# Splitting a shared expert block into three fp32r products of high and low parts, on a kernel of eight layers

## The chip, the cores and the metric

The kernel runs on one core of a Trainium2 chip. The metric is the device time of one execution in microseconds. Five engines matter: TensorE (PE; its weight loads are listed as PEld), VectorE (DVE), ScalarE (ACT), GpSimd (POOL) and SyncE (SP), which issues most of the transfers.

## What is computed

Four layers, each a gated attention and a gated feed-forward part, act on 2048 tokens (8 sequences of 256) of width 256. The change lies in the first feed-forward part: eight routed experts, two of them for each token, and a shared expert for every token.

```python
def _L0_ffn_ref(x, Wg, W1, b1, W2, b2, Ws1, bs1, Ws2, bs2):
    ...
    logits = xf @ Wg
    top_vals, top_idx = jax.lax.top_k(logits, TOP_K)
    top_w = jax.nn.softmax(top_vals, axis=-1)
    combine = jnp.zeros((T, N_EXPERTS), x.dtype).at[jnp.arange(T)[:, None], top_idx].add(top_w)
    h = jax.nn.relu(jnp.einsum('td,edf->tef', xf, W1) + b1)
    sparse = jnp.einsum('te,tef,efd->td', combine, h, W2)
    sparse = sparse + combine @ b2
    shared = jax.nn.relu(xf @ Ws1 + bs1) @ Ws2 + bs2
    out = sparse + shared
    ...
x = x + jnp.tanh(g_ffn[0]) * _L0_ffn_ref(_layernorm(x, axis=-1), ...)
```

Ws1 is 256x1024 and Ws2 1024x256. The kernel's line numbers below are those of the profile.

## The kernel before

Everything here happens in phase_experts with l = 0. Tokens are held in 16 tiles of 128, or 4 blocks of 512 (blk 0 to 3); x_tok holds the residual rows, xnT the normalised rows turned (width on the partitions, two halves k), xn_tok the normalised rows for the next part (in the buffer vbuf). The order of each engine is written out by hand, and semaphores join the engines.

1. The router's work, and on PE the shared expert for token blocks 0 and 1 (shared_block, L1503 and L1514).
2. The ring: 39 steps, each of 128 rows that are routed to one expert. In a step PE multiplies by the expert's first weights (L1557), ACT adds the bias and applies relu (L1442), PE turns the rows of the next step (L1546), ACT copies them (L1436), PE multiplies by the second weights (L1567), DVE adds a bias row (L1278), and POOL gathers the rows of a later step and scatters the result rows by indirect transfers (L1385, L1389). Steps 0 to 7 are written out, the others run in a loop.
3. Behind the ring PE runs the shared expert for token block 2, turns the normalised rows of blocks 0 and 1 (norm_T, L1580), runs the shared expert for token block 3, folds three small matrices for the next part, and turns the rows of blocks 2 and 3. ACT applies bias and relu to each of the eight hidden tiles f of 128 features by 512 tokens (L1423), which PE leaves in four PSUM banks in turn, and copies the turned rows out of PSUM (L355).
4. Meanwhile SP loads the scattered result rows back, a token block at a time (load_result, L1343), into two buffers gat, which lie in prob and probT. DVE's order is combine(0), norms(0), combine(1), norms(1), combine(2), combine(3), then shared_block and norms for block 2 and for block 3. combine (L1287) adds the weighted result rows to x_tok in eight passes of 128x256. shared_block adds the shared expert's rows from PSUM (L1261) and a bias row (L1266). norms takes statistics (L252 to L272), waits for POOL's power step (L277), and writes the normalised rows in four passes (L286).
5. POOL's order behind the ring is: three small products own_block for the fold (L1404), then the power step of norms for each block. A barrier ends the phase.

A matrix product of fp32 operands shows in the trace as two PE instructions, one of fp32r operands (a rounded 32-bit format) as one. The very last phase (L3171 to L3261) already works in three fp32r products: ACT writes a high part rounded to fp32r (L3189, L3196), DVE subtracts it from the full value to get the low part (L3213, L3218), and PE adds high times high, high times low and low times high (L3248 for the first layer, L3259 for the second).

Of the kernel before, what the change touches and what calls it, by code (L numbers as in the profile page):

```python
# [19 lines left out]
P = 128  # L20
NBATCH, SEQ, D = 8, 256, 256
T = NBATCH * SEQ
NT = T // P
BLK = 512
NB = T // BLK
KD = D // P
# [61 lines left out]
def decoder_kernel(nc, a, out):  # L88
    ctx = ExitStack()
    with ctx:  # L90
# [920 lines left out]
        def phase_experts(l, func, gi, keep, prefetch):  # L1011
# [78 lines left out]
            b2_sb = ts  # L1090

            def hidden(f):

                return ps[:, f % 4, 0:FINE]

            def normalised(blk, t):

                return xn_tok[:, blk * 4 + t, :]
            gat = [prob[:, :, :, :, :].rearrange("p a b c s -> p (a b c) s"), probT[:, :, :, :].rearrange("p a b s -> p (a b) s")]

# [21 lines left out]
            with nc.Block() as block:  # L1122
                @block.vector
                def _(dve):
# [149 lines left out]
                    def ring_step(s, v, k, last):  # L1274
                        dve.wait_ge(y_full[v], k + 1)
                        dve.wait_ge(y_st[v], k * 16)
                        dve.wait_ge(ld_b[v], k * 32 + 32)
                        dve.tensor_tensor(y_sb[v], ps[:, 4 + v, 0:D], b2_sb[:, v, :], ALU.add).then_inc(y_out[v], 1)  # L1278

                    def combine(blk):  # L1280
# [94 lines left out]
                def _(pool):  # L1375
# [11 lines left out]
                    def scatter(s):  # L1387
                        pool.wait_ge(y_out[s % 2], s // 2 + 1)
                        pool.indirect_dma_start(a["yg"], bass.IndirectOffsetOnAxis(dst_row[:, s:s + 1], 0), y_sb[s % 2], None).then_inc(y_st[s % 2], 16)  # L1389

                    pool.wait_ge(sent, 16)
                    pool.wait_ge(link, marks["indexed"])
# [4 lines left out]
                    for s in range(steps):  # L1397
                        if s + 3 < steps:
                            pool.wait_ge(g_full, s + 2)
                            gather(s + 3)  # L1400
                        scatter(s)
                    if shared:
                        for i in range(3):
                            ins = pool.tensor_tensor(own_block[i].rearrange("p (j c) -> p j c", c=HD), rep[:, i, :].unsqueeze(1).broadcast_to([P, GH, HD]),  # L1404
                                                     hmask[:, :].unsqueeze(2).broadcast_to([P, GH, HD]), ALU.mult)
                        ins.then_inc(wbd, 1)
                    for blk in range(NB):
                        nrm.power(pool, blk, 0)

                @block.scalar  # L1410
                def _(act):
# [26 lines left out]
                    def ring_step(s, v, k, last):  # L1438
                        act.wait_ge(ld_b[v], k * 32 + 32)
                        for f in range(NF):  # L1440
                            act.wait_ge(h_full, (s + lead) * NF + (f + 1))
                            act.activation(hs[:, f, :], hidden(f), func, bias=b1_sb[:, v, f:f + 1]).then_inc(h_in, 1)  # L1442
                        if not last:
                            rows_in(s + 1)

                    def norm_T(blk):
# [19 lines left out]
                    for blk in range(NB):  # L1466
                        if blk % 2 == 0:
                            shared_block(lead + steps + blk // 2, hT)
                        if shared and blk == 2:
# [8 lines left out]
                def _(pe):  # L1478
# [19 lines left out]
                    def shared_block(blk, u, hT):  # L1498
# [9 lines left out]
                        for tp in range(2):  # L1508
                            wait(pe, s_in, blk * 2)
                            for t in range(2):  # L1510
                                for f in range(NF):
                                    if tp == 0 and t == 0:
                                        pe.wait_ge(h_in, u * NF + (f + 1))
                                    ins = pe.matmul(ps[:, 4 + tp, t * D:(t + 1) * D], hT[:, f, (2 * tp + t) * P:(2 * tp + t + 1) * P],  # L1514
                                                    w2[0][:, f, :], start=(f == 0), stop=(f == NF - 1))
                            ins.then_inc(s_full, 1)

# [103 lines left out]
                    for blk in range(NB):  # L1621
                        if shared and blk % 2 == 0:
                            shared_block(lead + blk // 2, lead + steps + blk // 2, hT)
                        if shared and blk == 2:
# [1773 lines left out]
```

## Time and profile before

| | us |
|---|---|
| median of 3 runs | 1590.52 |
| lowest and highest | 1587.04, 1593.61 |
| profiled execution, its own time | 1590.82 |
| its span in the profile | 1588.3 |
| PE busy | 1393.3 (88%) |
| weight loads busy | 1125.8 (71%) |
| DVE busy | 698.4 (44%) |
| ACT busy | 653.1 (41%) |
| POOL busy | 486.8 (31%) |

The busy shares are averages over stages with different limits. In the profile the ring runs from about 312 to 597 us, and the part behind it, up to the barrier, from 597 to 664 us. All times below are microseconds from the start of the span.

### The profile page before, as it was taken

What the parts mean: (1) busy time and instruction counts of PE and PEld (TensorE: products, weight loads), DVE (VectorE), ACT (ScalarE), POOL (GpSimd) and SP (SyncE); (2) the same over time, 40 slices, a digit from 0 to 9 for tenths busy, and PEclk for the clock granted to TensorE, in tenths of its full rate; (3) what the DMA queues carried; (4) which work ended last, traced back from release to release, by engine and by line L of the source; (5) the groups of instructions that cost most, each with busy time, mean ns of one, the idle gap of its engine ahead of it and who ended that gap; (6) DMA issues with size and microseconds to landing.
All of it is one profiled execution on the core that took longest, in us unless ns stands there. A gap on an engine that the chain in (4) does not pass through costs nothing. (4 is left out here: it accounts for less than half of the span.)

```text
span 1588.3 us, 29051 instructions
## 1 busy us (share of the span) xinstructions
PE 1393.3 (88%) x9586; PEld 1125.8 (71%) x9587; DVE 698.4 (44%) x2242; ACT 653.1 (41%) x1466; POOL 486.8 (31%) x551
## 2 busy tenths in 40 slices
PE   4999978999999999799997899948588898686598
PEld 3666756699999996577776799945456777555587
DVE  4666725300000006277743300046654564459575
ACT  3354533244444442246662344433343444323352
POOL 4456531022222211213411022225237534031330
PEclk9899998999999999879998999978699999888799
DMA  8500006366666643000005465620137873010000
GB/s 280 163 2 1 2 1 218 117 197 201 198 203 195 205 152 119 7 14 15 15 8 150 163 212 189 209 66 1 36 133 228 285 222 113 1 53 1 1 26 26
DMA packets 114126, 175.84 MB, mean 111 GB/s; under 512 B 20555, under 2 KB 90845, under 8 KB 113513
## 3 DMA queue, kind: packets, MB, share of 16 engines
q1 hardware_dynamic: 103855, 146.35, 29.3%
q0 software_dynamic: 10176, 28.24, 4.9%
q8 instruction: 57, 0.93, 0.3%
q14 instruction: 38, 0.31, 0.1%
HBM read 135.16 MB, written 39.35 MB: 110 GB/s over the span
## 5 line engine op out<-in xcount | busy, mean ns | idle before, releaser
L1442 ACT ACTIVATE kT<-ps,b_sb 128x128 f32<-128x128 f32 x312 | 114.8, 368 | 155.6 <-PE ps L1557 134.7
L718 ACT ACTIVATE wbuf<-ps 128x512 f32<-128x512 f32 (+1 forms) x256 | 123.6, 542 | 85.6 <-PE ps L963 85.2
L1557 PEld LDWEIGHTS ps<-qT,wbuf 128*128 128x128 f32 x1248 | 145.4, 192 | 3.9 <-issue 1.9
L1557 PE MATMUL ps<-qT,wbuf 128*128 128x128 f32 x1248 | 145.7, 275 | 1.7 <-issue 1.7
L1567 PE MATMUL ps<-L0f_second,kT 128*128 x624 | 141.1, 379 | 0.0
L277 POOL TENSOR_TENSOR sm<-sm,mhalf 128x4 f32<-128x4 f32 (+1 forms) x40 | 45.0, 1124 | 292.2 <-DVE sm L272 292.2
L1567 PEld LDWEIGHTS ps<-L0f_second,kT 128*128 128x128 f32 x624 | 115.5, 190 | 14.1
L963 PE MATMUL ps<-nmT_r,sel_r 32*128 32x256 f32 (+1 forms) x512 | 110.9, 429 | 0.0
L765 DVE CUSTOM_DVE_ANT_0 ps<-ps,ts 128x128 f32<-128x128 f32 (+1 forms) x256 | 83.1, 391 | 44.3 <-PE ps L939 44.2
L768 DVE TENSOR_REDUCE nmax<-ps 128x2 f32<-128x512 f32 x128 | 80.5, 684 | 32.8 <-PE ps L939 32.7
L1968 ACT ACTIVATE kT<-ps,b_sb 128x128 f32<-128x128 f32 x152 | 55.6, 368 | 72.8 <-PE ps L2055 62.8
L355 ACT ACTIVATE xnT<-ps 128x512 f32<-128x512 f32 x64 | 36.4, 595 | 116.5 <-PE ps L332 63.8
L1385 POOL DMA_INDIRECT qT<-expert_rows,rowt x39 | 38.0, 974 | 149.0 <-PE ps L1546 106.4
L939 PE MATMUL ps<-hbuf,qT 32*128 32x512 f32 (+1 forms) x256 | 72.3, 687 | 3.4 <-POOL hbuf L613 1.2
L2055 PEld LDWEIGHTS ps<-qT,wbuf 128*128 128x128 f32 x608 | 70.9, 192 | 3.1 <-ACT qT L1962 1.5
L2055 PE MATMUL ps<-qT,wbuf 128*128 128x128 f32 x608 | 71.3, 275 | 1.6 <-ACT qT L1962 1.1
L959 PE MATMUL ps<-qT,hbuf 32*128 32x256 f32 (+1 forms) x512 | 72.4, 386 | 0.0
L1278 DVE TENSOR_TENSOR oT<-ps,ts 128x256 f32<-128x256 f32 x20 | 8.5, 425 | 139.8 <-PE ps L1567 139.8
L2065 PE MATMUL ps<-wbuf,kT 128*128 x304 | 68.8, 379 | 0.0
L959 PE MATMUL ps<-stage,hbuf 32*128 32x256 f32 (+1 forms) x512 | 68.2, 374 | 0.2 <-ACT nmT_r L675 0.2
L623 POOL TENSOR_SCALAR_AFFINE_SELECT wbuf<-wbuf 128x256 f32<-128x256 f32 x128 | 49.9, 411 | 57.4 <-ACT wbuf L718 55.5
L939 PE MATMUL ps<-hbuf,stage 32*128 32x512 f32 (+1 forms) x256 | 67.0, 569 | 0.0
(455 smaller groups left out, 3146.0 us busy)
## 6 DMA issues: line engine op xcount, KB each, us to landing
wbuf<-in_L_w SPq DMA_DIRECT2D x66, 1024.0 KB, 5.1
tree_rows<-rt SPq DMA_DIRECT2D x3, 3151.0 KB, 23.2
prob<-tree_rows SPq DMA_DIRECT2D x69, 137.0 KB, 3.7
tree_outputs<-probT SPq DMA_DIRECT2D x69, 128.0 KB
L0f_second<-in_L_w SPq DMA_DIRECT2D x8, 1024.0 KB, 11.5
ts<-in_L_b SPq DMA_DIRECT2D x58, 128.0 KB, 3.0
wbuf<-in_L_rec SPq DMA_DIRECT2D x3, 2048.0 KB, 9.3
expert_rows<-vbuf SPq DMA_DIRECT2D x2, 2048.0 KB, 12.3
```

Of the source, the lines that this page charges most:

```text
L718: act.activation(PT[:, k, :, q0:], ps[:, a_bank("ST", b, k), :].rearrange("p (h s) -> p h s", h=2)[:, :, q0:], ACT.Exp, scale=scale).then_ ...
L765: ins = dve.tensor_tensor_reduce(out=bank[:, e, 0:kk], in0=bank[:, e, 0:kk], in1=seen[:, SEQ - kk:SEQ], scale=-1.0, scalar=BIG, op0=ALU.ad ...
L768: ins = dve.tensor_reduce(nmax[:, b % 2, qt, h:h + 2], bank[:, :, 0:keys(qt)], AXX, ALU.max, negate=True)
L939: ins = pe.matmul(bank[:, :, 0:kk], qTb[blk % 2][r, g, u * SEQ + qt * P:u * SEQ + (qt + 1) * P], kmb[blk % 2][r, :, g, u * SEQ:u * SEQ + k ...
L959: pe.matmul(out, kmb[blk % 2][r, e, g, u * SEQ + kt * P:u * SEQ + (kt + 1) * P], qTb[blk % 2][r, g, u * SEQ + q0:(u + 1) * SEQ], start=Tru ...
L963: ins = pe.matmul(out, sel_r[r, h:h + 1].broadcast_to([2 * HD, P]), nmT_r[b % 2][r, q0:], start=False, stop=True)
L1442: act.activation(hs[:, f, :], hidden(f), func, bias=b1_sb[:, v, f:f + 1]).then_inc(h_in, 1)
L1557: ins = pe.matmul(hidden(f), first[v][:, kk, f * P:(f + 1) * P], xgT[:, kk, :], start=(kk == 0), stop=(kk == KD - 1))
L1567: ins = pe.matmul(ps[:, 4 + v, 0:D], hs[:, f, :], second[:, ds(e, 1), f * D:(f + 1) * D][:, 0, :], start=(f == 0), stop=(f == NF - 1))
L1968: act.activation(hs[:, f, :], hidden(f), func, bias=b1_sb[:, v, f:f + 1]).then_inc(h_in, 1)
L2055: ins = pe.matmul(hidden(f), first[v][:, kk, f * P:(f + 1) * P], xgT[:, kk, :], start=(kk == 0), stop=(kk == KD - 1))
L2065: ins = pe.matmul(ps[:, 4 + v, 0:D], hs[:, f, :], second[:, ds(e, 1), f * D:(f + 1) * D][:, 0, :], start=(f == 0), stop=(f == NF - 1))
```

## The change

For the shared expert on token blocks 2 and 3 alone, shared_block on PE and ACT is replaced by split_block. Each fp32 product becomes three fp32r products: high weights with high rows, high weights with low rows, low weights with high rows, 48 of 512 columns in the first layer and 96 of 256 columns in the second.

- The weights' high parts (hi_room, in prob and probT) are written by ACT in ring steps 2 to 5, the low parts by DVE in the same steps, over the weights themselves (wbuf 0).
- The high rows of block 2 are written by ACT in ring step 6, and the low rows by POOL behind the scatter of step 10 (low_rows(0)). Those of block 3 follow behind the ring: ACT behind the eight tiles of block 2, POOL behind the power step of norms(0) (low_rows(1)).
- For each hidden tile ACT writes the full value into one of four raw buffers and then its high part (hh), and POOL subtracts to get the low part (hl). PE's second layer waits for hid_lo, a tile at a time, and ACT waits for it before it writes a raw buffer again.
- On POOL low_hidden(0), the eight subtractions for block 2, stands ahead of the own_block products and of the first power step; low_hidden(1) stands ahead of the power step of norms(2).
- gat moves from prob and probT to the buffer of the ring's first weights (wbuf 1).

```diff
+            hi_room = nc.alloc_sbuf_tensor_at(f"{n}high", [P, 4096], F32R, offset=places["prob"])[:, :]
+            (hi1, lo1) = (x[:, 0:2048].rearrange("p (k f) -> p k f", k=KD) for x in (hi_room, wbuf_r[0]))
+            (hi2, lo2) = (x[:, 2048:4096].rearrange("p (f d) -> p f d", f=NF) for x in (hi_room, wbuf_r[0]))
+            hh, hl = (x.rearrange("p (f t) -> p f t", f=NF) for x in (wbuf_r[2], hbuf_r))
+            raw = attw[:, 0].rearrange("p w k n -> p (w k n)").rearrange("p (i t) -> p i t", i=4)
+            xh = [x.rearrange("p (k t) -> p k t", k=KD) for x in (rounded("rowsF", 4 * D, 1024), rounded("qT", 0, 1024))]
+            xl = [x.rearrange("p (k t) -> p k t", k=KD) for x in (rounded("stage", 0, 1024), rounded("kT", 0, 1024))]
...
-            gat = [prob[:, :, :, :, :].rearrange("p a b c s -> p (a b c) s"), probT[:, :, :, :].rearrange("p a b s -> p (a b) s")]
+            gat = [wbuf[:, 1, v * 2048:(v + 1) * 2048].rearrange("p (t d) -> p t d", d=D) for v in range(2)]
...
                         dve.tensor_tensor(y_sb[v], ps[:, 4 + v, 0:D], b2_sb[:, v, :], ALU.add).then_inc(y_out[v], 1)
+                        if isinstance(s, int) and 2 <= s < 6:
+                            q = chunk(s - 2)
+                            dve.wait_ge(w_hi, s - 1)
+                            dve.tensor_tensor(wbuf_r[0][:, q], wbuf[:, 0, q], hi_room[:, q], ALU.subtract).then_inc(w_lo, 1)
...
+                    def low_rows(i):
+                        pool.wait_ge(x_hi, i + 1)
+                        pool.tensor_tensor(xl[i], xnT[:, :, block_of(i)], xh[i], ALU.subtract).then_inc(x_lo, 1)
+
+                    def low_hidden(i):
+                        for f in range(NF):
+                            pool.wait_ge(hid_hi, i * NF + f + 1)
+                            pool.tensor_tensor(hl[:, f, :], raw[:, f % 4, :], hh[:, f, :], ALU.subtract).then_inc(hid_lo, 1)
...
                         scatter(s)
+                        if s == 10:
+                            low_rows(0)
                     if shared:
+                        low_hidden(0)
                         for i in range(3):
...
                     for blk in range(NB):
                         nrm.power(pool, blk, 0)
+                        if blk == 0:
+                            low_rows(1)
+                        elif blk == 1:
+                            low_hidden(1)
...
+                        if isinstance(s, int) and 2 <= s < 6:
+                            q = chunk(s - 2)
+                            act.wait_ge(s_full, 2 * lead)
+                            act.activation(hi_room[:, q], wbuf[:, 0, q], ACT.Identity).then_inc(w_hi, 1)
+                        if isinstance(s, int) and s == 6:
+                            act.activation(xh[0], xnT[:, :, block_of(0)], ACT.Identity).then_inc(x_hi, 1)
+
+                    def split_block(i):
+                        for f in range(NF):
+                            act.wait_ge(h_full, (lead + steps + i) * NF + (f + 1))
+                            wait(act, hid_lo, i * NF + f - 3)
+                            act.activation(raw[:, f % 4, :], ps[:, f % 4, :], func, bias=col("L0_bs1", f)).then_inc(h_in, 1)
+                            act.wait_ge(h_in, (lead + steps + i) * NF + (f + 1))
+                            act.activation(hh[:, f, :], raw[:, f % 4, :], ACT.Identity).then_inc(hid_hi, 1)
+                        if i == 0:
+                            act.activation(xh[1], xnT[:, :, block_of(1)], ACT.Identity).then_inc(x_hi, 1)
...
-                            shared_block(lead + steps + blk // 2, hT)
+                            split_block(blk // 2)
...
+                    def split_block(i):
+                        u = lead + steps + i
+                        pe.wait_ge(x_lo, i + 1)
+                        pe.wait_ge(w_lo, 4)
+                        for f in range(NF):
+                            if f >= 4:
+                                pe.wait_ge(h_in, u * NF + (f - 3))
+                            for k in range(KD):
+                                for j, (w, x) in enumerate(((hi1, xh[i]), (hi1, xl[i]), (lo1, xh[i]))):
+                                    ins = pe.matmul(ps[:, f % 4, :], w[:, k, f * P:(f + 1) * P], x[:, k, :],
+                                                    start=(k == 0 and j == 0), stop=(k == KD - 1 and j == 2))
+                            ins.then_inc(h_full, 1)
+                        for tp in range(2):
+                            pe.wait_ge(s_in, (lead + i) * 2)
+                            for t in range(2):
+                                for f in range(NF):
+                                    if tp == 0 and t == 0:
+                                        pe.wait_ge(hid_lo, i * NF + (f + 1))
+                                    for j, (h, w) in enumerate(((hh, hi2), (hh, lo2), (hl, hi2))):
+                                        ins = pe.matmul(ps[:, 4 + tp, t * D:(t + 1) * D], h[:, f, (2 * tp + t) * P:(2 * tp + t + 1) * P],
+                                                        w[:, f, :], start=(f == 0 and j == 0), stop=(f == NF - 1 and j == 2))
                             ins.then_inc(s_full, 1)
...
-                            shared_block(lead + blk // 2, lead + steps + blk // 2, hT)
+                            split_block(blk // 2)
```

In the prediction block 0 and block 1 of the split are token blocks 2 and 3, the first and the second behind the ring; combine and norms are numbered by token block.

## Rows read from the trace of the kernel before

**Rows 1.** Stretches: busy us of PE, PEld, DVE, ACT, POOL (instructions), granted clock, DMA.
```profile
597.20:625.00 27.80, 27.76 (x98) 18.44 (x99) 16.71 (x55) 5.50 (x8) 4.14 (x6) 1.00 0.53 170
...
661.60:663.70 2.10, 1.97 (x8) 1.57 (x8) 0.06 (x1) 0.60 (x1) 0.00 (x0) 0.50 0.00 0
1487.40:1490.80 3.40, 3.39 (x8) 2.72 (x9) 0.00 (x0) 0.43 (x1) 3.40 (x2) 0.52 0.00 0
1490.90:1499.70 8.80, 8.80 (x40) 7.28 (x39) 5.27 (x6) 8.28 (x14) 3.81 (x2) 1.00 0.00 0
```

**Rows 2.** Timeline of PE behind the ring: start, us, instruction, count, [idle before].
```profile
597.24 13.97 PE L1503 MATMUL ps<-xnT,wbuf 128*128 128x512 f32 x32 [0.61 <-DVE oT L1278]
...
624.86 1.04 PE L1580 MATMUL ps<-ident,vbuf 128*128 128x128 f32 x8
...
627.14 13.90 PE L1503 MATMUL ps<-xnT,wbuf 128*128 128x512 f32 x32
...
661.71 1.97 PE L1580 MATMUL ps<-ident,vbuf 128*128 128x128 f32 x8 [2.59 <-DVE vbuf L286]
```

**Rows 3.** Timeline of PE in the last phase, in three products.
```profile
1526.38 0.40 PE L3259 MATMUL ps<-wbuf_r,wbuf_r 128*128 128x256 f32 x2
...
1535.01 0.40 PE L3248 MATMUL ps<-ctxT_r,wbuf_r 128*128 x1
...
1545.92 0.40 PE L3259 MATMUL ps<-wbuf_r,wbuf_r 128*128 128x256 f32 x2
```

**Rows 4.** Timeline: ACT behind the ring; ACT and DVE in the last phase.
```profile
599.23 0.69 ACT L1423 ACTIVATE hbuf<-ps,cols 128x512 f32<-128x512 f32 x1 [5.65 <-PE ps L1503]
...
1497.44 0.69 ACT L3194 ACTIVATE hbuf<-ps,cols 128x512 f32<-128x512 f32 x1
...
1498.83 0.69 DVE L3218 TENSOR_TENSOR hbuf_r<-hbuf,wbuf_r 128x512 fp32r<-128x512 f32 x1 [0.67 <-ACT wbuf_r L3196]
```

**Rows 5.** Groups of POOL instructions by shape: count | busy us, mean ns | idle before.
```profile
L634 POOL TENSOR_SCALAR xs<-x_tok,sm 128x256 f32<-128x256 f32 x32 | 38.9, 1222 | 1.7
...
L613 POOL TENSOR_SCALAR hbuf<-ctxT,sel 128x512 f32<-128x512 f32 x14 | 21.8, 1573 | 55.2 <-PE ps L963 47.7 <-POOLq L114 7.5
...
L2140 POOL TENSOR_TENSOR probT<-rowsF,bmask 128x512 f32<-128x512 f32 x4 | 5.1, 1268 | 6.3 <-SPq L2131 6.3
```

**Rows 6.** Timeline of POOL, then of DVE, at one place of the last phase.
```profile
1515.28 2.38 POOL L3171 TENSOR_TENSOR vbuf<-vbuf,rowsF 128x1024 f32 x1
1517.62 2.59 POOL L3171 TENSOR_TENSOR x_tok<-x_tok,rowsF 128x1024 f32 x1
...
1515.49 5.00 DVE L305 SCALAR_TENSOR_TENSOR x_tok<-ts,sm,x_tok 128x256 f32 x2 [0.35 <-POOL sm L277]
```

**Rows 7.** Timeline of POOL and DVE at the start of the third attention.
```profile
1076.79 1.26 POOL L2140 TENSOR_TENSOR probT<-rowsF,bmask 128x512 f32<-128x512 f32 x1 [6.31 <-SPq L2131]
...
1076.81 1.53 DVE L2186 TENSOR_SCALAR rowsA<-rowsA,gates 128x512 f32<-128x512 f32 x1 [7.69 <-PEq L114]
```

**Rows 8.** Timeline of POOL and DVE behind the ring.
```profile
598.36 1.11 POOL L1404 TENSOR_TENSOR attw<-rep,hmask 128x128 f32<-128x128 f32 x3
...
605.53 3.38 DVE L1287 SCALAR_TENSOR_TENSOR x_tok<-prob,r,x_tok 128x256 f32<-128x256 f32 x8 [8.44 <-DMA prob<-expert_outputs]
...
612.55 1.38 DVE L286 TENSOR_SCALAR vbuf<-x_tok,sm 128x256 f32<-128x256 f32 x4 [1.16 <-POOL sm L277]
...
620.81 1.38 DVE L286 TENSOR_SCALAR vbuf<-x_tok,sm 128x256 f32<-128x256 f32 x4 [1.13 <-POOL sm L277]
...
654.89 0.88 DVE L1261 SCALAR_TENSOR_TENSOR x_tok<-ps,gates,x_tok 128x256 f32<-128x256 f32 x2 [5.11 <-PE ps L1514]
```

**Rows 9.** Timeline: ACT and POOL in a ring step; ACT rounding weights in a later phase.
```profile
358.30 3.44 ACT L1442 ACTIVATE kT<-ps,b_sb 128x128 f32<-128x128 f32 x8 [3.54 <-PE ps L1557]
...
347.33 0.97 POOL L1385 DMA_INDIRECT qT<-expert_rows,rowt  x1 [2.32 <-PE ps L1546]
...
1450.54 1.06 ACT L2988 ACTIVATE wbuf_r<-wbuf 128x1024 fp32r<-128x1024 f32 x1
```

More of the change, by code:

```diff
@@ L1090, in phase_experts, with chunk, block_of @@
             b2_sb = ts
+            w_hi, w_lo, x_hi, x_lo = (psem(n + x) for x in ("w_hi", "w_lo", "x_hi", "x_lo"))
+            hid_hi, hid_lo = psem(n + "hid_hi"), psem(n + "hid_lo")
+            hi_room = nc.alloc_sbuf_tensor_at(f"{n}high", [P, 4096], F32R, offset=places["prob"])[:, :]
[5 more added lines that the diff above has]
+            xl = [x.rearrange("p (k t) -> p k t", k=KD) for x in (rounded("stage", 0, 1024), rounded("kT", 0, 1024))]
+            def chunk(j):
+                return slice(j * 1024, (j + 1) * 1024)
+            def block_of(i):
+                return slice((lead + i) * BLK, (lead + i + 1) * BLK)
             def hidden(f):
@@ L1515, in shared_block @@
                                                     w2[0][:, f, :], start=(f == 0), stop=(f == NF - 1))
+                            ins.then_inc(s_full, 1)
+                    def split_block(i):
[19 more added lines that the diff above has]
+                                                        w[:, f, :], start=(f == 0 and j == 0), stop=(f == NF - 1 and j == 2))
                             ins.then_inc(s_full, 1)
```

## The prediction

> **What bounds the kernel now.** I read the page first (which engine is busiest), then the stretch that the change rewrites, engine by engine in order of time, then the one other place that already multiplies in high and low parts, and last the rows where POOL and VectorE (DVE) work at once. TensorE (PE) sets the time through the routed ring and through the shared block of the first token block behind it: that block's two layers follow each other without a gap [rows 2] at a granted clock of 1.00 [rows 1], and DVE's addition to x_tok then waits for PE [rows 8]. So an instruction saved on PE there counts, as long as PE is not made to wait. Between the two shared blocks that is close: PE must turn the normalised rows of blocks 0 and 1, and DVE finishes those of block 1 at 620.81 + 1.38 = 622.2 [rows 8], only 2.7 us before PE's first block ends at 624.9 [rows 2]. DVE is the engine next in line, and this change leans on DVE's neighbour.
>
> **PE's work.** One fp32 block takes 624.86 - 597.24 = 27.6 us [rows 2]. The last phase has the same shapes in three fp32r products: its first layer takes 1545.92 - 1535.01 = 10.9 us, and its second, in the stretch where nothing waits, 1535.01 - 1526.38 = 8.63 us for 24 of its 32 groups, so 0.36 us a group and 11.5 us in all [rows 3]. A new block is 22.4 us, a gain of 5.2 us each, 10.4 us for both. That is all there is to win.
>
> **What moves into the ring costs nothing.** ACT writes the high weight parts in steps 2 to 5 and the first high rows in step 6, 128x1024 each; such a pass took 1.06 us and ACT waits 3.54 us in every step [rows 9]. DVE's four low weight parts are 128x1024; a 128x512 subtraction took 0.69 us [rows 4], so 1.4 us at most, and DVE does nothing else in a step but one addition (queued behind it: the next addition, a step later). On POOL low_rows(0) stands behind scatter 10 and ahead of gather 14; POOL idles 2.32 us before a gather [rows 9], the subtraction is some 2.4 us, and the gathered rows are read over a step later. If that cover failed, one gather late by 0.1 us would be the price. The result rows now land in the first layer's weight buffer, which the ring has left when those loads are issued; their place in SP's queue is the same. The waits on x_lo (first block) and w_lo are long met.
>
> **POOL's subtractions, block 0.** Times are on the clock of the profile before. PE starts at 597.24 and gives a tile of hidden rows every 10.9 / 8 = 1.36 us. ACT started 0.25 us after the first tile was complete (599.23, four instructions of 0.44 after 597.24 [rows 2, 4]); from the first ACT pass to the subtraction it is 1498.83 - 1497.44 = 1.39 us [rows 4]. So subtraction f can start at 597.24 + 1.36 + 0.25 + 1.39 = 600.24 plus 1.36 f. No POOL row writes fp32r. The nearest is POOL's f32 two-input pass of this size, 1.27 us; the far ends are 1.57 us (one input and a pointer) and 1.22 us for half the size, 2.44 us [rows 5]. None below 1.27 at this size, so no gain. I take 1.26, since DVE's fp32r and f32 passes of one size cost alike, and keep 2.44 for the range. Alone, POOL would then keep up: subtraction 7 ends at 611.0, PE has reached its group 7 at 610.7, and next to nothing is lost.
>
> **POOL against DVE.** It is not alone. While POOL added rows at 1515.28 and 1517.62, two DVE passes of 0.42 us took 5.00 us: each ended when a POOL pass had ended, one pass after the other, and the second POOL pass was 0.21 us longer than the first [rows 6]. A DVE tensor_scalar started beside a POOL pass of 1.26 us took 1.53 us, 0.29 past its end [rows 7]. So two-input DVE passes and DVE's scalar passes from SBUF to SBUF take turns with POOL. DVE's combine(0) (8 such passes) starts at 605.53, when its rows land [rows 8], as subtraction 3 ends. From there a POOL pass and a DVE pass alternate, 1.26 + 0.28 = 1.54 us a pair: subtraction 7 ends at 605.58 + 4 x 1.54 = 611.7. Behind it on POOL stand the three own_block products (0.37 each [rows 8]), three more turns, 1.95 us; combine(0) ends at 614.0, not 608.9. The power step of norms(0) stands behind all this on POOL; with the same distance as before (612.55 - 608.91) it ends at 617.6. Right behind it in POOL's queue is low_rows(1), 2.4 us (128x1024 [rows 6]), ready by then; POOL starts it before DVE starts (1515.28 against 1515.49 behind a power step [rows 6]), and DVE's normalising passes wait: they end at 617.6 + 2.4 + 1.4 = 621.4, not 613.9. From there to the normalised rows of block 1 it is as before, 622.19 - 613.93 = 8.3 us [rows 8]: 629.7, which is 7.5 us late.
>
> The Trainium skill's "SBUF — State Buffer", section "Who interferes with whom", says the same of that pair: DVE's second port is shared with GpSimd under an exclusive lock held for a whole instruction, and passes with two SBUF inputs or in a 2-port mode take it. It speaks against this change; by it the sum is the +1.1 us below, without it the -7.9 us of the second rival, and the rows side with it.
>
> **PE again.** Block 0's first layer ends at 608.2; group 7 waits for 611.8, then 0.36 + 8.63: block 0 ends at 620.8, 4.1 us early. Then PE waits for DVE until 629.7. After a wait of 2.59 us the turning took 1.97 us against 1.04 [rows 2], at a granted clock of 0.50 [rows 1], the lower of the two levels, so block 1 starts at 631.7, not 627.14. In the last phase the low level lasted for 8 products of 0.43 instead of 0.23 us [rows 1]; 1.6 us in all; part of it falls on the turning, so I take 0.7 us, an estimate. First layer to 643.3; subtraction f at 631.7 + 0.7 + 3.0 + 1.36 f. DVE is then in combine(2) and combine(3) (629.7 to 638.7 with turns) and in shared_block's four two-input additions; about six subtractions are stretched from 1.36 to 1.54 us, so the last ends at 644.9 + 1.26 + 0.8 = 646.9. PE: 647.0 + 0.36 + 8.63 = 656.0. Before, it was 27.6 us after 627.14, 654.8, and DVE's last addition at 654.89. The power of norms(2) now stands behind the subtractions (it ends at 649), but PE needs those rows only after 656. **Sum: +1.1 us** (4.1 us gained, 8.6 lost between the blocks, 3.4 gained in block 1), handed on unchanged, since everything behind waits for this. Profiled 1590.82 + 1.1 = 1591.9; the median of the runs lies 0.3 lower: 1591.6.
>
> **Rivals.** *Slower: POOL writes fp32r slowly.* The decider is the time of one 128x512 subtraction. At 1.57 us, the same steps give subtraction 7 at 614.2, block 1's normalised rows at 632.8, PE's end at 661.9, +7 us. At 2.0 us, subtraction 7 at 617.7, rows at 637, block 1's last subtraction at 660.5, its end at 669.6, +14.7 us or 1605; it passes 8 us at about 1.6. For it: POOL's pointer forms show such rates, and four raw buffers make ACT wait for POOL. Against: the two-input form does not. *Faster: DVE is not held.* If POOL and DVE overlap freely, power 0 waits only for the own_block products (612.2, not 611.5), block 1's rows are ready at 622.9, PE goes on at 624, and block 1 ends 13.9 + 9.0 us later at 646.9: -7.9 us, 1582.6. Against: every row of rows 6 and 7. *In between*, DVE may win more turns, or the normalising passes go first: 1 to 3 us less, in my own range.
>
> **How the numbers follow.** The forecast, 1588 to 1597 (one POOL pass between 1.2 and 1.5 us, the clock 1.5 us either way), gets 0.69; the slower rival 0.15, spread over 1597 to 1610; the faster one 0.11, 1582 to 1588; 0.05 for a delay not foreseen. The measurement tells 0.5%, 8 us: below 1582.6 lies 0.04, above 1598.5 lies 0.12, within 0.84. The range cuts the outer parts of both rivals: 1584 to 1601.
>
> **What would show it.** Right: POOL's subtractions at 1.25 us and stretched from the fifth on; combine(0) some 8 us long instead of 3.4; PE idle about 7 us ahead of block 1's turning, which runs at the lower clock level; PE's blocks without their waits at 22.4 us. Wrong: a subtraction of over 1.6 us, DVE passes of 0.42 us beside POOL, ring steps longer than before, or a first layer not at 1.36 us a tile.

## The result, and the profile after

| | before | after |
|---|---|---|
| median of 20 runs each, us | 1590.55 | 1593.61 |
| lowest and highest | 1584.94, 1593.63 | 1585.73, 1599.21 |
| ratio, 95% interval | | 1.0022 [1.0012, 1.0032] |
| profiled execution, its own time | 1590.82 | 1594.28 |
| its span | 1588.3 | 1592.4 |
| POOL busy | 486.8 | 517.8 |

The changed kernel is no faster: slower by 3.5 us, between 1.9 and 5.1, which lies inside the 0.5% that the prediction called no change. The prediction, 1591.6 us within 1584 to 1601, holds the time, but some 2 us of the difference come from a place that it did not look at.

For all that follows, *the stage* runs from the first product of the shared block behind the ring to VectorE's first instruction behind the barrier. In the kernel before that is 597.24 [rows 2] to 667.75, 70.5 us; its end there:

```profile
667.75 0.35 DVE L825 TENSOR_SCALAR rowsA<-rowsA,gates 128x256 f32<-128x256 f32 x1 [6.09 <-PEq L114]
```

The timeline of the kernel after, PE, then POOL, then DVE (start, us, engine, line, operation, count, [idle time before and who ended it]):

```profile
597.71 0.47 PE L1579 MATMUL ps<-rowsF_r,L0f_high 128*128 128x512 f32 x1 [0.56 <-issue]
...
612.11 0.39 PE L1589 MATMUL ps<-L0f_high,wbuf_r 128*128 128x256 f32 x1 [0.76 <-POOL hbuf_r L1418]
...
629.40 1.97 PE L1655 MATMUL ps<-ident,vbuf 128*128 128x128 f32 x8 [7.15 <-DVE vbuf L286]
...
600.80 11.26 POOL L1418 TENSOR_TENSOR hbuf_r<-attw,wbuf_r 128x512 fp32r<-128x512 f32 x8 [1.94 <-ACT wbuf_r L1494]
612.02 1.67 POOL L1436 TENSOR_TENSOR attw<-rep,hmask 128x128 f32<-128x128 f32 x3
616.52 1.05 POOL L277 TENSOR_TENSOR sm<-sm,mhalf 128x4 f32<-128x4 f32 x1 [2.83 <-DVE sm L272]
617.56 2.39 POOL L1413 TENSOR_TENSOR kT_r<-xnT,qT_r 128x1024 fp32r<-128x1024 f32 x1
...
606.14 7.83 DVE L1307 SCALAR_TENSOR_TENSOR x_tok<-wbuf,r,x_tok 128x256 f32<-128x256 f32 x8 [8.54 <-DMA wbuf<-expert_outputs]
...
617.61 3.47 DVE L286 TENSOR_SCALAR vbuf<-x_tok,sm 128x256 f32<-128x256 f32 x4 [1.17 <-POOL sm L277]
...
627.96 1.38 DVE L286 TENSOR_SCALAR vbuf<-x_tok,sm 128x256 f32<-128x256 f32 x4 [1.13 <-POOL sm L277]
...
656.07 0.88 DVE L1277 SCALAR_TENSOR_TENSOR x_tok<-ps,gates,x_tok 128x256 f32<-128x256 f32 x2 [3.97 <-PE ps L1589]
...
668.97 0.35 DVE L825 TENSOR_SCALAR rowsA<-rowsA,gates 128x256 f32<-128x256 f32 x1 [6.13 <-PEq L114]
```

Read it against [rows 8]. combine(0), 3.38 us before, takes 7.83 us; it starts while POOL is in its eight subtractions and ends 0.3 us behind POOL's last small product. Normalising block 0, 1.38 us before, takes 3.47 us: the first of its four passes ends only 0.15 us behind low_rows(1) on POOL, which ends at 619.96. So block 1's rows are ready at 629.3, and PE stands idle for 7.15 us before it turns them. What the faster products won is given back in that wait and in the low clock behind it: PE's second block ends 58.2 us into the stage, before it was 57.5. The stage ends after 668.97 - 597.71 = 71.3 us, 0.8 us longer than before.

The granted clock belongs to it. Stretches of the kernel after (us, busy us of PE, PEld, DVE, ACT and POOL with their counts, granted clock, DMA):

```profile
597.71:608.68 10.97, 10.97 (x49) 9.09 (x49) 2.54 (x3) 9.07 (x14) 8.59 (x7) 1.00 0.65 196
608.68:621.20 12.52, 11.76 (x97) 11.55 (x96) 11.14 (x23) 2.47 (x4) 8.45 (x8) 1.00 0.41 122
...
629.40:631.00 1.60, 1.60 (x8) 1.60 (x9) 1.56 (x5) 0.45 (x1) 0.00 (x0) 0.50 0.00 0
631.00:634.60 3.60, 3.60 (x11) 2.83 (x10) 3.53 (x9) 1.38 (x3) 0.00 (x0) 0.50 0.00 0
```

Block 2's products take 10.97 and 12.52 us at a granted clock of 1.00, with 0.76 us of waiting: 22.7 us instead of the 27.6 of [rows 2]. The clock falls during the wait and is at 0.50, the lower level of 1.2 GHz, until about 634.6; the second block's first layer takes 643.69 - 631.02 = 12.7 us instead of 11.

### The profile page after: what moved, and what is told of

Read it like the earlier page. It is cut to its first block and busy times, and to the rows that moved or that the text cites. A ratio compares the mean times of both kernels' runs of the same rounds, so it can differ in the third digit from the quotient of the medians.

```text
span 1592.4 us, 29301 instructions
## 1 busy us (share of the span) xinstructions
PE 1386.7 (87%) x9682; PEld 1133.0 (71%) x9683; DVE 714.6 (45%) x2246; ACT 669.0 (42%) x1488; POOL 517.8 (33%) x569
## 5 line engine op out<-in xcount | busy, mean ns | idle before, releaser
L2130 PEld LDWEIGHTS ps<-qT,wbuf 128*128 128x128 f32 x608 | 70.9, 192 | 3.1 <-ACT qT L2037 1.5
L2130 PE MATMUL ps<-qT,wbuf 128*128 128x128 f32 x608 | 71.3, 275 | 1.6 <-ACT qT L2037 1.1
L623 POOL TENSOR_SCALAR_AFFINE_SELECT wbuf<-wbuf 128x256 f32<-128x256 f32 x128 | 50.2, 415 | 57.0 <-ACT wbuf L718 55.2
L959 PE MATMUL ps<-stage,hbuf 32*128 32x256 f32 (+1 forms) x512 | 68.2, 374 | 0.2 <-ACT nmT_r L675 0.2
```

The source lines that it names most:

```text
L959: pe.matmul(out, kmb[blk % 2][r, e, g, u * SEQ + kt * P:u * SEQ + (kt + 1) * P], qTb[blk % 2][r, g, u * SEQ + q0:(u + 1) * SEQ], start=Tru ...
L2130: ins = pe.matmul(hidden(f), first[v][:, kk, f * P:(f + 1) * P], xgT[:, kk, :], start=(kk == 0), stop=(kk == KD - 1))
```

## The experiments

One table first. The wait of ScalarE is the one for the last store in the tree phase, which comes up in the second half. Where no ratio stands, there was one profiled execution, and only the parts read from its trace are compared, since single times of one kernel lie up to 13.5 us apart. Each ratio is to the kernel before as it was run beside that kernel, with medians of 1588.97 to 1590.55 us; so the medians of two rows are not to be subtracted.

| kernel | stage, us | ScalarE's wait | median, us | ratio to before |
|---|---|---|---|---|
| before | 70.5 | 3.66 | 1590.55 | |
| after | 71.3 | 5.72 | 1593.61 | 1.0022 [1.0012, 1.0032] |
| e1, no subtractions for block 2 | 67.4 | 5.73 | | |
| e2, low rows early | 69.2 | 5.23 | | |
| e3, own_block products late | 70.9 | 5.35 | | |
| e6, fills for subtractions | 67.3 | 5.08 | | |
| e7, VectorE subtracts | 67.6 | 5.55 | | |
| e9, new order, POOL subtracts | 64.8 | 5.53 | | |
| e8, new order, VectorE subtracts | 63.2 | 5.42 | 1587.78 | 0.9979 [0.9965, 0.9993] |
| b_order, before in the new order | 68.2 | 3.67 | 1588.48 | 0.9992 [0.9976, 1.0007] |
| e10, subtractions earlier | 60.7 | 5.17 | 1583.78 | 0.9959 [0.9944, 0.9973] |
| e11, the ring's additions alone | 70.6 | 3.61 | 1590.66 | 1.0005 [0.9990, 1.0020] |
| b_eps, other last bits | 70.5 | 3.68 | 1591.03 | 1.0006 [0.9990, 1.0023] |
| e12, as e10, 62 instructions more | 62.5 | 3.67 | 1581.20 | 0.9950 [0.9931, 0.9968] |

### Is it the subtractions on POOL? (e1)

```diff
-                        low_hidden(0)
...
-                                    for j, (h, w) in enumerate(((hh, hi2), (hh, lo2), (hl, hi2))):
+                                    for j, (h, w) in enumerate(((hh, hi2), (hh, lo2), (hl if i else hh, hi2))):
```

> Left out: POOL's eight subtractions for the first split block; PE's second layer there waits for the high parts alone and multiplies the high part once more in place of the low part. Everything else is as in the changed kernel, whose stage (first product of the first split block to the first DVE instruction behind the barrier) took 71.3 us, against 70.5 before the change. Theory (POOL's reading passes and DVE's two-input passes take turns): combine(0) takes 3.4 us instead of 7.8, the power step of norms(0) comes 3.6 us behind its end, the normalising passes still take 3.5 us behind low_rows(1), the normalised rows of block 1 are ready 4.4 us earlier, and the stage takes 66.8 us, within 0.7. Rival (DVE is late for another reason, its rows landing late or PE's own pace): 70.5 to 71.3 us.

ScalarE, too, no longer waits for POOL before it writes a raw buffer of that block. Timeline of that kernel, DVE, POOL and PE:

```profile
606.50 3.38 DVE L1307 SCALAR_TENSOR_TENSOR x_tok<-wbuf,r,x_tok 128x256 f32<-128x256 f32 x8 [8.66 <-DMA wbuf<-expert_outputs]
613.52 3.48 DVE L286 TENSOR_SCALAR vbuf<-x_tok,sm 128x256 f32<-128x256 f32 x4 [1.17 <-POOL sm L277]
...
613.48 2.39 POOL L1413 TENSOR_TENSOR kT_r<-xnT,qT_r 128x1024 fp32r<-128x1024 f32 x1
...
625.32 1.97 PE L1655 MATMUL ps<-ident,vbuf 128*128 128x128 f32 x8 [3.83 <-DVE vbuf L286]
```

combine(0) takes 3.38 us again, as in [rows 8], and the stage 67.4 us: as the theory had it. The 2.1 us that low_rows(1) takes from the normalising passes are still there.

### Which POOL pass costs what? (e2, e3)

e2 issues low_rows(1) ahead of power(0):

```diff
+                        if blk == 0:
+                            low_rows(1)
                         nrm.power(pool, blk, 0)
-                        if blk == 0:
-                            low_rows(1)
-                        elif blk == 1:
+                        if blk == 1:
                             low_hidden(1)
```

> One move on POOL: low_rows(1) stands ahead of the power step of norms(0) instead of behind it, in the gap in which POOL waited 2.8 us for DVE's statistics. Theory: DVE's four normalising passes of block 0 take 1.4 us instead of 3.5, nothing else is held, block 1 starts 2.1 us earlier and the stage takes 69.2 us instead of 71.3. Rival (the hold only moves, because the subtraction now runs into combine(0) or into the power step): 70.8 to 71.5 us.

```profile
615.13 2.58 POOL L1413 TENSOR_TENSOR kT_r<-xnT,qT_r 128x1024 fp32r<-128x1024 f32 x1
...
619.72 1.38 DVE L286 TENSOR_SCALAR vbuf<-x_tok,sm 128x256 f32<-128x256 f32 x4 [1.16 <-POOL sm L277]
...
629.43 1.97 PE L1655 MATMUL ps<-ident,vbuf 128*128 128x128 f32 x8 [5.71 <-DVE vbuf L286]
```

Beside the statistics the same POOL pass holds almost nothing (only the first two-input pass there, L260, waits for its end: 0.81 us instead of 0.17), normalising takes 1.38 us again, and the stage is 69.2 us, on the number expected. e3 moves the three own_block products from behind low_hidden(0) to behind power(2):

> One move on POOL: the three own_block products stand behind the power step of norms(2), where the fold still gets them in time, instead of between the subtractions and the first power step. Theory: three turns less for combine(0), 7.8 us become 6.0, the rows of block 1 are ready 1.8 us earlier, the stage takes 69.5 us. Rival (the subtractions alone set the end of combine(0)): 71.0 us or more.

```profile
600.48 11.11 POOL L1418 TENSOR_TENSOR hbuf_r<-attw,wbuf_r 128x512 fp32r<-128x512 f32 x8 [1.96 <-ACT wbuf_r L1495]
...
605.42 7.63 DVE L1307 SCALAR_TENSOR_TENSOR x_tok<-wbuf,r,x_tok 128x256 f32<-128x256 f32 x8 [8.15 <-DMA wbuf<-expert_outputs]
```

A miss. combine(0) is 0.2 us shorter and the stage 0.3, not 1.8. Here the subtractions end at 611.59 and combine(0) at 613.05; its last three passes take 0.47 us each. In the kernel after they took 0.62, in turns with the three products of 0.58 us. A turn with a POOL pass about as short as the DVE pass costs little; I had charged each turn as if it came on top.

### Does POOL hold VectorE because it is busy, or because it reads? (e6)

```diff
-                            pool.tensor_tensor(hl[:, f, :], raw[:, f % 4, :], hh[:, f, :], ALU.subtract).then_inc(hid_lo, 1)
+                            pool.memset(hl[:, f, :].bitcast(F32), 0.0).then_inc(twice, 1)
+                            pool.wait_ge(twice, i * NF + f + 1)
+                            pool.memset(hl[:, f, :].bitcast(F32), 0.0).then_inc(hid_lo, 1)
```

> Left out: every subtraction of POOL for the hidden tiles; in its place two fills of the same 128x512 low part with zeros, one after the other, some 1.1 us together by the fills of the trace (942 ns for 1024 columns), so POOL is as busy and in the same order, but reads nothing. If DVE's two-input passes are held only by a POOL pass that reads, combine(0) takes 3.4 to 4.5 us (the three own_block products still read), the rows of block 1 are ready 3 to 4 us earlier, and the stage takes 67 to 68 us instead of 71.3. If any POOL pass holds them: combine(0) 6.5 us or more and 70 us or more.

```profile
608.36 0.53 POOL L1421 MEMSET hbuf_r<- 128x512 f32 x1
609.13 0.53 POOL L1419 MEMSET hbuf_r<- 128x512 f32 x1 [0.25 <-ACT wbuf_r L1497]
...
607.64 3.38 DVE L1308 SCALAR_TENSOR_TENSOR x_tok<-wbuf,r,x_tok 128x256 f32<-128x256 f32 x8 [8.48 <-DMA wbuf<-expert_outputs]
```

POOL writes through that stretch, two fills in every 1.36 us, and combine(0) takes 3.38 us. That the fills are short is not the reason: beside the own_block products, which read and take 0.58 us, VectorE's passes took 0.62 us in the kernel after, and 0.47 without them in e3. So here a POOL pass that reads SBUF holds VectorE's two-input passes, one that only writes does not. The Trainium skill, "SBUF — State Buffer", section "Who interferes with whom", draws the same line, between GpSimd instructions that read SBUF and those that only write it; here it is 7.83 against 3.38 us.

### The same work on the other engine (e7)

VectorE does the eight subtractions of block 2, four in its idle time ahead of combine(0) and four between its passes, and low_rows(1) in its wait for power(1).

```diff
+                    for f in range(4):
+                        low(0, f)
+                    combine(0, [(0, f) for f in range(4, NF)])
+                    norms(0)
+                    combine(1)
+                    norms(1, (low_rows,))
```

> The same subtractions on the other engine. VectorE makes the eight low hidden parts of the first split block (four in its idle time ahead of combine(0), four between the passes of combine(0)) and the low rows of the second block (in its wait for power(1)); POOL makes only the low hidden parts of the second block. Stage = from the first product of the split block behind the ring to VectorE's first instruction behind the barrier (before 70.5 us, after 71.3). Theory (POOL's reading passes alternate with VectorE's two-input passes): a subtraction alone on VectorE takes half of the 1.22 us that its 128x1024 one in the ring takes, some 0.65 us, so combine(0) and its four subtractions take 3.4 + 2.6 = 6 us, normalising takes 1.4 us again, TensorE waits 3 to 4 us instead of 7.15 for the second block's rows, and the stage takes 67.2 to 68.5 us, 3 to 4 under that of after. Rival (the work is too much for VectorE, the hold was no loss): combine(0) with its subtractions as long as before the move, 7.8 us or more, stage 70 us or more.

```profile
609.21 0.68 DVE L1302 TENSOR_TENSOR hbuf_r<-attw,wbuf_r 128x512 fp32r<-128x512 f32 x1
609.82 0.87 DVE L1316 SCALAR_TENSOR_TENSOR x_tok<-wbuf,r,x_tok 128x256 f32<-128x256 f32 x2
...
614.80 1.38 DVE L286 TENSOR_SCALAR vbuf<-x_tok,sm 128x256 f32<-128x256 f32 x4 [1.16 <-POOL sm L277]
...
625.41 1.97 PE L1671 MATMUL ps<-ident,vbuf 128*128 128x128 f32 x8 [3.93 <-DVE vbuf L286]
```

As expected: a subtraction of 128x512 is 0.68 us on VectorE, combine(0) with four of them 5.6 us (605.63 to 611.2) instead of 7.83 without any, and the stage 67.6 us. Here the engine that lent its neighbour the work and then waited for it in turns paid more than the work. PE still waits 3.93 us, so the question became whether it must turn rows there at all.

### The order of the stage (b_order, e9, e8, e10)

Nothing that the second shared block reads is written by the turning of blocks 0 and 1, so nothing asks for the turning between the blocks. In these kernels PE and ACT run both blocks and turn only then:

```diff
+                    for i in range(2):
+                        split_block(i)
                     for blk in range(NB):
-                        if shared and blk % 2 == 0:
-                            split_block(blk // 2)
```

b_order does that alone, in the kernel before, with shared_block.

> The kernel before with TensorE's and ScalarE's order alone changed: both fp32 shared blocks behind the ring one after the other, then the turning. Theory: before, TensorE loses only the 2 us of turning between the two blocks and some of their clock, so the two blocks end after 2 x 27.6 = 55.2 us instead of 57.6, and the stage takes 67.5 to 69 us instead of 70.5: 1.5 to 3 us faster. It says what of the new order's gain belongs to the products of high and low parts. Rival (turning is paid again behind the blocks): 70 us or more, no change.

```profile
599.70 13.97 PE L1503 MATMUL ps<-xnT,wbuf 128*128 128x512 f32 x32 [0.61 <-DVE oT L1278]
...
654.87 1.04 PE L1580 MATMUL ps<-ident,vbuf 128*128 128x128 f32 x8
...
667.91 0.35 DVE L825 TENSOR_SCALAR rowsA<-rowsA,gates 128x256 f32<-128x256 f32 x1 [6.09 <-PEq L114]
```

The stage ran from 599.70 to 667.91, 68.2 us, 2.3 us less, as expected. Over the whole time that stays inside the interval. e9 has the new order with POOL subtracting (VectorE makes low_rows(1), runs combine(1) in its wait for power(0), and adds block 2's rows ahead of combine(2)):

> The order of the stage changed: TensorE and ScalarE run the second split block right behind the first and turn the rows of the token blocks only then; VectorE runs combine(1) inside its wait for power(0), the adds of the first split block ahead of normalising(1), and the low rows of the second block; POOL still makes both blocks' low hidden parts. Stage as for the other runs (before 70.5 us, after 71.3). Theory: TensorE's wait of 7.15 us and its low clock behind it are gone, but POOL's subtractions now hold combine(0) (about 7.8 us instead of 3.4) and combine(2) and (3) too, so VectorE becomes the engine that sets the end: stage 65 to 68 us. Rival (the holds cost nothing once TensorE doesn't wait): as the kernel in which VectorE subtracts, 60 to 62 us.

```profile
625.56 10.86 POOL L1435 TENSOR_TENSOR hbuf_r<-attw,wbuf_r 128x512 fp32r<-128x512 f32 x8
...
630.02 5.27 DVE L286 TENSOR_SCALAR vbuf<-x_tok,sm 128x256 f32<-128x256 f32 x4
...
662.51 0.35 DVE L825 TENSOR_SCALAR rowsA<-rowsA,gates 128x256 f32<-128x256 f32 x1 [6.13 <-PEq L114]
```

64.8 us, nearer to the theory than to its rival: VectorE's normalising is held again, 5.27 us instead of 1.38, now by the second block's subtractions. e8 gives all sixteen to VectorE:

> The order of the run in which POOL subtracts, but VectorE makes all sixteen low hidden parts itself, between the passes of combine(0), (2) and (3). Theory: TensorE runs both split blocks without a wait (2 x 22.4 = 45 us), VectorE's chain (combines 13.5, subtractions in the way some 8, statistics and normalising 4 x 4, adds 7) ends about together with it, and the last block's adds, statistics, normalising, turning and the barrier take their 13 us: stage 60 to 62 us, 8 to 10 under before, some 1582 us against 1590.5. Rival (VectorE becomes the bound with sixteen more passes): stage 64 to 67 us and no gain over the run in which POOL subtracts.

```profile
634.76 0.39 PE L1605 MATMUL ps<-L0f_high,wbuf_r 128*128 128x256 f32 x1 [0.96 <-DVE hbuf_r L1302]
...
661.22 0.35 DVE L825 TENSOR_SCALAR rowsA<-rowsA,gates 128x256 f32<-128x256 f32 x1 [6.13 <-PEq L114]
```

63.2 us, between the two: PE's second layer waits for VectorE's last subtractions, which I had put behind passes that nobody was waiting for. e10 makes these first:

```diff
+                    def second_lows():
+                        for f in range(4):
+                            low(1, f)
+                        dve.wait_ge(sadd, 2 * lead + 2)
+                        combine(2, [(1, f) for f in range(4, NF)], 1)
...
+                    norms(1, (lambda: shared_block(2), second_lows))
+                    combine(3)
+                    norms(2, (lambda: shared_block(3),))
```

> As the kernel in which VectorE makes all sixteen low hidden parts, whose second block's second layer waited until 637.4 us for the last of them: here the second block's eight come right after the adds of the first split block, the last four one behind each pass of combine(2), ahead of combine(3); and the last block's adds lie in the wait for power(2). Theory: TensorE runs the second block in 22.4 us again instead of 27.4, VectorE's chain loses one wait for a power (1.2 us), and the stage takes 60 to 61.5 us instead of 63.2 (before 70.5): the whole time 2 to 3 us under that kernel's, if the tree phase is the same. Rival (VectorE's chain alone sets the end, the order of its passes doesn't matter): 62.5 us or more.

Stretches of that kernel, PE first; they are its two blocks:

```profile
597.58:620.40 22.82, 22.47 (x142) 20.39 (x143) 17.11 (x45) 11.53 (x17) 4.04 (x5) 1.00 0.55 165
620.40:643.00 22.60, 22.60 (x148) 20.70 (x147) 20.59 (x59) 10.59 (x16) 1.32 (x2) 1.00 0.13 44
```

Behind them, PE's first turning and VectorE's first instruction behind the barrier:

```profile
643.08 1.04 PE L1672 MATMUL ps<-ident,vbuf 128*128 128x128 f32 x8
...
658.29 0.35 DVE L825 TENSOR_SCALAR rowsA<-rowsA,gates 128x256 f32<-128x256 f32 x1 [6.13 <-PEq L114]
```

Two blocks of 22.6 to 22.8 us with next to no gap (0.35 us in the first), at a granted clock of 1.00, and a stage of 60.7 us, within the expected 60 to 61.5. That is 9.8 us under the kernel before, where the order alone, with fp32 blocks, gave 2.3. PE's two blocks take 45.5 us there and 55.2 in b_order, so on PE the products of high and low parts are worth 9.7 of the 10.4 us that the prediction counted. At the end of the stage 7.5 us of it are left. The 7.5 are not theirs alone: e10 also changed VectorE's order, which was not tried with fp32 blocks.

### Where the other 2 us went (e11, b_eps, e12)

The stage accounts for 0.8 of after's 3.5 us. The barriers of the profile show where the rest is: of the later phases only the second feed-forward part, the tree phase, is over half a microsecond longer. It is a ring of row loads and stores, and its length swings: 243.8 to 247.1 us in the four kernels with plain fp32 blocks, 245.0 to 250.6 in the first nine with split blocks. One wait at its end is steadier. Timeline of ScalarE, which waits for the last store, in the kernel before:

```profile
1322.38 1.09 ACT L2734 ACTIVATE qT<-ps 128x512 f32<-128x512 f32 x2 [3.66 <-DMA tree_outputs<-probT]
```

and after:

```profile
1326.98 1.08 ACT L2809 ACTIVATE qT<-ps 128x512 f32<-128x512 f32 x2 [5.72 <-DMA tree_outputs<-probT]
```

It is 3.6 to 3.7 us in those four kernels, 5.1 to 5.7 in those nine. e11 keeps the change's additions to the ring and runs the blocks in plain fp32 on the old weights; b_eps is the kernel before with every activation changed in its last bits (EPS = 1.1e-5).

> The change's additions to the ring alone (the high and low parts of the weights and of the first block's rows are made there, the gather's room is moved), with the two shared blocks behind the ring in plain fp32 on the weights as they were, so that every number is that of the kernel before; no subtractions of hidden parts. Theory (the ring hides its additions; the part of the change's time that the stage doesn't explain comes from the tree phase, and there from something else than these additions): ring as long as before, stage 70.5 +- 0.5 us, tree phase 243.8 to 244.5 us, whole time as before within its interval. Rival A (the additions, or the program that they lengthen, slow the tree phase): tree phase 246 us or more, 2 to 3 us slower. Rival B (the additions lengthen the ring): the ring over 0.5 us longer.

> The kernel before with the norms' constant at 1.1e-5 instead of 1e-5: every instruction the same, every activation behind the first norm changed in its last bits, as the three products change them too. Theory D (the change's longer tree phase comes from other last bits, through which rows go to other places): tree phase 245 us or more, and 15 us instead of 13.5 from the last load of a step's rows to the gather of the third tree. Theory P (it comes from the program, not from the numbers): tree phase 243.8 to 244.5 us, 13.5 us, whole time as before.

Both took the time of the kernel before within their intervals, and waited 3.61 and 3.68 us at that spot. So it is neither the additions nor the numbers. e11's ring was as long as before and its stage 70.6 us; its tree phase of 247.1 us would by itself have spoken for its rival A, and that of b_eps, about 244.8 us, lies between what its two theories expected. So the phase's length is no measure; the wait is.

What the nine share is 192 more PE instructions (9682 products and 9683 weight loads against 9586 and 9587) and two more waits. Transfer queues of the kernel after, from 1 us into that wait to its end (queue, kind: packets, MB, share):

```profile
q1 hardware_dynamic: 394, 1.13, 68.2%
q8 instruction: 1, 0.02, 2.1%
```

In all nine a packet of the instruction queue moves in that stretch, in none of the four. e12 tests that by length alone:

```diff
+                    for _ in range(122):
+                        pe.wait_ge(gate_in, 8)
```

> As the fastest kernel so far (stage 60.7 us, 1583.78 us), with 122 met waits, which make 62 instructions, at the end of TensorE's queue in the first experts phase, where it waits some 5 us for the barrier. What is open: at the end of the tree phase ScalarE waits 5.1 to 5.7 us for the last store in all nine kernels with split blocks and 3.6 to 3.7 us in the four without, and only in the nine does a packet of the instruction queue move between that store and its landing. These nine have 194 more instructions for TensorE (14907 instead of 14713, and 57 packets, so some 258 a packet); with 62 more the shift is 256, nearly a whole packet, and the packet should move some 4 to 5 us earlier, to where it moved before. Theory (that packet holds the last store or the loads around it up): the wait is 3.6 to 3.7 us again, no such packet moves in that stretch, 13.5 to 13.7 us from the last load of a step's rows to the third gather instead of 14.95, the whole time 1 to 2 us less. Rival (the packet is only a companion): the packet moves away, the wait stays over 5 us. The 62 instructions lie beside the other engines' end of the phase: stage 60.7 +- 0.5 us.

Timeline of ScalarE in e12:

```profile
1317.55 1.08 ACT L2828 ACTIVATE qT<-ps 128x512 f32<-128x512 f32 x2 [3.67 <-DMA tree_outputs<-probT]
```

The wait is 3.67 us again, and no instruction packet moves in that stretch; it moves from 1312.6 on, 1.3 us ahead of the wait, as in the kernel before. The theory holds: longer code in one phase changed when a later phase loads its code, and there a wait became 1.5 to 2.1 us longer.

The trace also shows what the packet does to the store, which is 128 packets of 1 KB. In the kernel after 120 of them have started by 1324.6. The instruction packet, 16 KB, moves from 1324.06 to 1325.64. Packets from 1324.60 to 1325.60, and from 1325.60 to 1326.40:

```profile
DMA packets 31, 0.25 MB, mean 254 GB/s; under 512 B 0, under 2 KB 0, under 8 KB 0
...
DMA packets 47, 0.32 MB, mean 399 GB/s; under 512 B 1, under 2 KB 9, under 8 KB 9
```

No packet of the store starts in the first stretch, where only the 1024 KB load issued behind it moves on. The store's last eight start in the second, from 1325.62 on. In each of the nine kernels exactly eight of the 128 come late, and the first of them starts within 0.02 us of the end of the instruction packet; in the four and in e12 none does. Eight of 128 is the share of one of the 16 DMA engines, so the instruction packet seems to stand ahead of them on one engine. The engine is inferred, the order in time is measured.

The 62 instructions were not free where I put them. VectorE waited 8.10 us for the barrier instead of 6.13, and the stage took 62.5 us. e12 is still the fastest, 0.9950 [0.9931, 0.9968] of before; over e10 its interval overlaps, so between the two nothing is shown but the wait.

Both causes together, the stage's difference plus the wait's difference, against what was timed:

| kernel | stage + wait, us | timed, us |
|---|---|---|
| after | 0.75 + 2.06 = 2.8 | 3.5 [1.9, 5.1] |
| e8 | -7.3 + 1.8 = -5.5 | -3.3 [-5.6, -1.1] |
| e10 | -9.8 + 1.5 = -8.3 | -6.5 [-8.9, -4.3] |
| e12 | -8.0 + 0.0 = -8.0 | -7.9 [-11.0, -5.1] |
| b_order | -2.3 + 0.0 = -2.3 | -1.3 [-3.8, 1.1] |

All five sums lie within the intervals, that of e8 at its edge. What they leave over, up to 2.2 us, stays open; the rest of the tree phase, which swings from one execution to the next, may hold it.

## Why the prediction was right, point by point

- **PE's blocks.** 22.4 us from [rows 3]; measured 22.6 to 22.8 where nothing waits. Right.
- **The ring hides its part.** From the start of the phase to the first product behind the ring it was 354.0 us before and 354.1 after, and e11 shows it apart. Right.
- **POOL's rate.** 1.26 us taken, from [rows 5]; the first four, which run alone, take 1.29 us each. So the slower rival, which needed 1.6 us, fell: 1.29 against 1.27 us, writing fp32r cost POOL next to nothing.
- **Turns.** Expected from [rows 6, 7]: combine(0) to end at 614.0. It ended at 613.97, where the split block started 0.47 us later, so 0.5 us earlier than forecast. The subtractions stretched from the fifth on, to between 1.45 and 1.55 us. Normalising was held for 2.1 us by low_rows(1), where 2.4 had been counted. e1, e2, e6 and e7 show that these turns cost what was said. The three small turns were taken at 1.95 us; the three products took 1.67, and without them combine(0) gained only 0.2 us (e3).
- **PE's wait.** About 7 us expected, 7.15 measured, and the turning took 1.97 us at 0.50.
- **The clock behind it.** Taken as 0.7 us of slow products, an estimate; the first layer was 1.7 us longer than at the full clock. A term that was mis-sized, by 1 us.
- **The sum in the stage.** +1.1 forecast, +0.8 measured. On PE block 0 gained 4.1 us as forecast; between the blocks 7.5 us were lost instead of 8.6, and block 1 gained 2.7 instead of 3.4. That the two errors lie against each other is luck.
- **"Handed on unchanged".** This step failed. Behind the barrier the change shifted the loading of code, and one wait in the tree phase became 2.1 us longer. That nothing computed there changes did not mean that nothing there could move. The range was wide enough for it; the sum had no such term, and that the measured time lay in the range says nothing for this step.
- **The faster rival** (no hold) was priced at -7.9 us for the given order. e6 frees both blocks of the subtractions' holds but keeps low_rows(1), and the stage reaches -3.3 us. The whole of -7.9 was not tried; with another order e10 went beyond it.

## What to carry to other kernels

Before work is given to an idle POOL, look at what VectorE does in those microseconds: here a POOL pass that reads SBUF and a two-input VectorE pass ran in turns, and the short one paid. Put the work where its reader's queue has slack, in the order in which it is waited for, and ask whether an engine must stop between two blocks at all. A difference that no stage explains may be the program's length: look for the instruction queue's packets beside the wait that grew.

## What the runs showed of the hardware

- Writing only: POOL fills of 0.53 us, two in every 1.36 us, left combine(0) at 3.38 us (e6).
- The same subtraction of 128x512 takes 0.68 us on VectorE (e7) and 1.29 us on POOL.
- One instruction packet of about 16 KB (0.93 MB in 57 packets before) was enough to lengthen a store's landing by 1.5 to 2.1 us: eight of the store's 128 packets started only when it had ended. 62 more instructions moved it away (e12). The Trainium skill, "Advanced Engine Details and Errata", section "ISA Cache", gives 16 KB and 256 instructions for a line; the shift of 194 + 62 that put the packet back agrees with it.
- The clock fell during PE's wait of 7.15 us. The lower level of 1.2 GHz still held for the 5.2 us of work behind it, 629.4 to 634.6, and cost about 1 us in the turning and 1.7 us in the products behind it.
